# Token 0 first through the feed-forward block, and the step index read earlier

## The reference, cut to what matters

```
def step(h, p):
    op = jnp.argmax(h[0, 0, :NOPS])                      # NOPS = 19
    q = h @ p['wq'][op]; k = h @ p['wk'][op]; v = h @ p['wv'][op]
    attn = softmax(einsum('bqd,bkd->bqk', q, k) * scale)
    y = einsum('bqk,bkd->bqd', attn, v) @ p['wo'][op]
    h = where(p['am'][op], y, h)
    z = relu(h @ p['w1'][op] + p['b1'][op]) @ p['w2'][op] + p['b2'][op]
    h = where(p['fm'][op], z, h)
```

## Time and profile before

| | us |
|---|---|
| median of 3 runs (lowest to highest) | 219.69 (218.63 to 220.36) |
| the profiled execution, its device time | 218.97 |
| the profiled execution, its span | 217.2 |
| TensorE products busy in the span | 171.0 (79%) |
| VectorE busy | 142.4 (66%) |
| ScalarE busy | 107.8 (50%) |
| POOL busy | 58.3 (27%) |

### The profile page before, as it was taken

The page is one execution under the profiler, slowest core; times in us unless marked ns, Lnnn a source line. Parts: engine busy times, 40 slices in busy tenths (PEclk is TensorE's granted clock), DMA queues, the critical chain, the costliest instruction groups (busy, mean ns, idle before and its releaser), DMA issues.

```text
span 217.2 us, 4109 instructions
## 1 busy us (share of the span) xinstructions
PE 171.0 (79%) x1197; PEld 116.4 (54%) x1199; DVE 142.4 (66%) x392; ACT 107.8 (50%) x318; POOL 58.3 (27%) x136
## 2 busy tenths in 40 slices
PE   8589969965594799989369499999684999998730
PEld 5554856532392577745242278677332787765310
DVE  0862265857957688893844478898755589787452
ACT  2334261237853566662577058676441576755330
POOL 8800000000060545561000004654600036555100
PEclk9999999999769589999956969999997599999985
DMA  6500000000000000000000000000000000000002
GB/s 210 199 0 3 0 3 1 2 0 5 0 0 0 3 0 3 0 0 0 10 11 6 18 0 0 0 0 0 0 0 14 0 0 0 0 0 0 0 0 98
DMA packets 2635, 3.18 MB, mean 15 GB/s; under 512 B 825, under 2 KB 1849, under 8 KB 2618
## 3 DMA queue, kind: packets, MB, share of 16 engines
q1 hardware_dynamic: 2330, 2.66, 3.9%
q10 hardware_dynamic: 288, 0.32, 0.5%
HBM read 2.45 MB, written 0.53 MB: 14 GB/s over the span
## 4 chain that ended last, share of the span: by engine, by line
PE 55%; DVE 19%; ACT 8%; issue 8%; DMA 3%; POOL 3%; DVEq 2%; ACTq 1%; SPq 1%; POOLq 0%
PE bank L502 15%; PE bank L475 8%; PE bank L489 4%; PE bank L466 4%; PE bank L728 4%; ACT qz L890 3%; PE bank L562 3%; PE bank L616 3%; PE bank L545 3%; DVE big L1168 3%; POOL prob L418 3%; DMA kx<-kx_dram 2%; DVE minus L1152 2%; DVE filt L331 2%; PE bank L766 2%
## 5 line engine op out<-in xcount | busy, mean ns | idle before, releaser
L418 POOL TENSOR_SCALAR prob<-prob,einv 128x256 f32<-128x256 f32 x96 | 44.9, 482 | 62.6 <-DVE einv L1163 62.6
L1168 DVE COPY big<-bank 128x512 f32<-128x512 f32 x48 | 32.9, 686 | 6.2 <-PE bank L475 6.1
L475 PE MATMUL bank<-ident,prob 128*128 128x128 f32 x192 | 31.2, 286 | 6.9 <-POOL prob L418 6.8
L807 ACT ACTIVATE prob<-bank,nmax 128x256 f32<-128x256 f32 x64 | 29.8, 472 | 12.8 <-DVE nmax L1155 12.8
L502 PE MATMUL bank<-hT,qz 128*128 128x256 f32 x128 | 33.6, 391 | 0.0
L475 PEld LDWEIGHTS bank<-ident,prob 128*128 128x128 f32 x192 | 22.2, 144 | 19.5 <-POOL prob L418 15.3
L502 PEld LDWEIGHTS bank<-hT,qz 128*128 128x128 f32 x128 | 23.2, 198 | 4.1 <-issue 1.6
L1155 DVE TENSOR_REDUCE nmax<-bank 128x2 f32<-128x512 f32 x32 | 21.7, 687 | 5.1 <-PE bank L502 4.6
L807 ACT ACTIVATE prob<-minus,nmax 128x256 f32<-128x256 f32 x32 | 15.9, 499 | 10.9 <-DVE nmax L1152 8.3
L502 PE MATMUL bank<-kt,qz 128*128 128x256 f32 x64 | 18.4, 419 | 3.2 <-ACT prob L807 3.2
L545 PE MATMUL bank<-ident,filt 128*128 128x128 f32 x96 | 12.2, 276 | 5.1 <-DVE big L1003 2.1
(11 more groups left out here) (161 smaller groups left out, 253.6 us busy)
## 6 DMA issues: line engine op xcount, KB each, us to landing
xrev<-xrev_dram SPq DMA_DIRECT2D x1, 512.0 KB, 5.3
xin<-xtok_dram SPq DMA_DIRECT2D x1, 512.0 KB, 5.2
out_dram<-outT SPq DMA_DIRECT2D x2, 256.0 KB, 2.3
wx<-wx_dram SPq DMA_DIRECT2D x1, 288.0 KB, 4.0
maskc<-maskc_dram SPq DMA_DIRECT2D x1, 256.0 KB, 4.9
kx<-kx_dram ACTq DMA_DIRECT2D x1, 248.0 KB, 4.1
constf<-constf_dram SPq DMA_DIRECT2D x1, 218.0 KB, 5.3
wa<-wa_dram SPq DMA_DIRECT2D x3, 56.0 KB, 1.8
```

The lines of the kernel that those rows point to most:

```text
L418: last = nc.gpsimd.tensor_scalar(prob[b % NPB][:, ih, :], prob[b % NPB][:, ih, :], einv[:, b, ih:ih + 1], 1.0, ALU.mult, ALU.mult)
L475: mm = pe.transpose(bank[2 + b % 2][:, jh * S + ih * P:jh * S + (ih + 1) * P], prob[b % NPB][:, ih, jh * P:(jh + 1) * P], ident)
L807: e = nc.scalar.activation(prob[b % NPB][:, ih, :], scores, ACT.Exp, bias=nmax[:, b, ih:ih + 1], scale=-1.0 if masked else 1.0, accum_out= ...
L1168: nc.vector.tensor_copy(flat(probT[b % NTB]), bank[2 + b % 2][:, :]).then_inc(s_PT, 1)
```

## The change

- A single column of the hidden layer, token 0's, is multiplied first, into column 0 of bank 7 (`TOKEN0`), ScalarE applies ReLU to it into a new tile `h0`, and TensorE multiplies `h0` with `w2` and adds the bias into columns 32 to 63 of bank 7, behind the first half of the hidden products. Three semaphores order this.
- `pick_op` on VectorE stands ahead of its ReLUs of both halves.
- The second half's fourth hidden product uses bank 7 (the third bank 3), and waits until VectorE has copied the row.
- TensorE calls `next_step` after the second half and ahead of the output products. VectorE calls it ahead of its last drain.
- ScalarE drains groups 0, 1 and 2, VectorE group 3 alone.

```diff
-        FF = "ADAD" + "ADAD" + "ADAD"
+        FF = "ADAD" + "ADAD" + "AAAD"
-        HBANK = ((0, 1, 4, 2), (5, 6, 7, 3))
+        HBANK = ((0, 1, 4, 2), (5, 6, 3, 7))
+        TOKEN0 = bank[7]
...
                     for q in range(GB):
                         rows = slice(q * C, (q + 1) * C)
+                        if (gp, q) == (1, GB - 1):
+                            pe.wait_ge(s_rowc, r)
                         pe.matmul(bank[HBANK[gp][q]][:, :], w1r[rows, :], flat(hT[rows, 2 * gp:2 * gp + 2, :]),
...
+                    pe.matmul(TOKEN0[:, 0:1], w1r[0:C, :], hT[0:C, 0, 0:1], start=True, stop=True,
+                              tile_position=(0, 0)).then_inc(s_h0, 1)
                     hidden(t, k0, 0)
+                    ffns = pe.snap(reg_ffns)
+                    pe.wait_ge(s_h0r, ffns)
+                    pe.matmul(TOKEN0[0:1, C:2 * C], h0[:, 0:1], w2s, start=True, stop=False)
+                    pe.matmul(TOKEN0[0:1, C:2 * C], b2s, ident[:, 0:C], start=False, stop=True).then_inc(s_row, 1)
+                    pe.reg_alu(reg_ffns, reg_ffns, 1, ALU.add)
...
                     hidden(t, k1, 1)
-
-                    t.drained(pe, k0 + 1)
-                    pe.matmul(bank[0][0:1, 0:C], relu[:, 0, 0, 0:1], w2s, start=True, stop=False)
-                    pe.matmul(bank[0][0:1, 0:C], b2s, ident[:, 0:C], start=False, stop=True).then_inc(s_row, 1)
+                    next_step(pe, b, reg_r, reg_op, reg_code)
                     for n in range(NG):
...
                         mm.then_inc(s_task, 1)
-                    next_step(pe, b, reg_r, reg_op, reg_code)
                     weight_products()
...
                     act.wait_ge(s_w1z, r)
+                    ffns = act.snap(reg_ffns)
+                    act.wait_ge(s_h0, ffns)
+                    nc.scalar.activation(h0[:, :], TOKEN0[:, 0:1], ACT.Relu, bias=b1s).then_inc(s_h0r, 1)
+                    act.reg_alu(reg_ffns, reg_ffns, 1, ALU.add)
...
-                    for n in (0, 2):
+                    for n in (0, 1, 2):
                         t.filled(act, k + n)
...
-                link(nc.vector.tensor_copy(row[:, :], bank[0][0:1, 0:C]))
+                nc.vector.tensor_copy(row[:, :], TOKEN0[0:1, C:2 * C]).then_inc(s_rowc, 1)
+                dve.wait_ge(s_rowc, r)
                 argmax_op(row[:, 0:NOPS])
...
+                    pick_op(r)
                     k = k0
                     for gp in range(2):
...
-                        if gp == 0:
-                            pick_op(r)
                         k += GB
-                    for n in (1, 3):
-                        t.filled(dve, k + n)
-                        nc.vector.tensor_scalar(hT[:, n, :], bank[ZBANK[n]][:, 0:S], b2s, None, ALU.add).then_inc(s_dd, 1)
                     next_step(dve, b, reg_r, reg_op, reg_code)
+                    n = NG - 1
+                    t.filled(dve, k + n)
+                    nc.vector.tensor_scalar(hT[:, n, :], bank[ZBANK[n]][:, 0:S], b2s, None, ALU.add).then_inc(s_dd, 1)
```

More of the change, by code:

```diff
@@ L200, in build @@
         wfs = sb("wfs", [HID, C + 2])
+        h0 = sb("h0", [HID, 1])
         w2s, b1s, b2s = wfs[:, 0:C], wfs[:, C:C + 1], wfs[:, C + 1:C + 2]
@@ L231, in build @@
             "step_weight_products_in_psum"), sem("step_block_weights_ready")
+        s_h0, s_h0r, s_rowc = sem("token0_hidden_in_psum"), sem("token0_hidden_ready"), sem("token0_copied")
         s_fin = sem("out_ready")
@@ L661, in _ @@
             pe.reg_mov(reg_att, B)
-            reg_wp = pe.alloc_register("pe_weight_products")
+            reg_wp, reg_ffns = pe.alloc_register("pe_weight_products"), pe.alloc_register("pe_ffns")
+            pe.reg_mov(reg_ffns, 1)
             pe.reg_mov(reg_wp, 0)
@@ L788, in _ @@
                     pe.wait_ge(s_dd, dd)
-                    pe.matmul(bank[0][0:1, 0:C], hT[:, 0, 0:1], ident[:, 0:C], start=True, stop=True).then_inc(s_row, 1)
+                    pe.matmul(TOKEN0[0:1, C:2 * C], hT[:, 0, 0:1], ident[:, 0:C], start=True, stop=True).then_inc(s_row, 1)
                     next_step(pe, b, reg_r, reg_op, reg_code)
@@ L917, in _ @@
             act.reg_mov(reg_task, len(STATIC))
+            reg_ffns = act.alloc_register("act_ffns")
+            act.reg_mov(reg_ffns, 1)
             reg_code, reg_op, reg_step, reg_kind, reg_r = (
```

## The result

The changed kernel takes **212.41 us** (median of 4 runs, 211.73 to 213.28) beside 220.01 (218.63 to 220.36) for the kernel before, a ratio of 0.967 [0.961, 0.972]. The forecast was 213.8, range 211.8 to 217.2. The profiled execution of the changed kernel took 213.28, its longest of four, with a span of 211.5; that of before 218.97, span 217.2. Both have 1.8 us outside the span, so the rows account for 5.7 us, and the rest of the 7.6 between the medians is which executions were profiled.

The account below looks back on a forecast made before the run. TensorE work set more than half of the span, with hollows where it waited for the late index. Gains of 1.3, 2.0 and 2.0 plus 0.6 for the clock, 5.9 us, off the median 219.69 gave 213.8, range 211.8 to 217.2.

Parts of the forecast that it names:

- Block 2: Second feed-forward block and change of step: earlier index lets weight products start 2.0 us earlier, directly behind the output products.
- The end: Last drain to final addition: drain 1.0 us earlier and VectorE's reading, taken as 1.0, no longer behind it; 2.0.
- TensorE's reading is covered: TensorE's register reads ahead of the outputs, taken as 1.0 us, hide behind its second half and VectorE's ReLU.
- the bound of 4.5: First half's output products starting later than 4.5 us after the block's first product would mean TensorE's reading isn't covered.
- The uncovered rival: TensorE reads registers only after the second half leaves the array, for 1.48 us: sum 2.7, 217.0 us; chance 0.13.
- its slower form: TensorE's reading takes longer than POOL's 1.48 us, each microsecond more costing three: 222.3 us; chance 0.05.
- VectorE's registers hold the diagonals: Changes of step: queries stay 2.55 us behind VectorE's last drain, 1.0 later in both: 215.8 us; chance 0.10.
- The clock: TensorE's half clock in attentions behind the blocks: busier TensorE holds full clock partly, a credit of 0.6 us.
- a hollow of 0.9: TensorE's idle gap remaining in front of the queries' products, a reason to take the clock credit nearer to zero.
- The bound of 1.9: Most a held clock could give back over both half-clock stretches, 0.65 + 1.21 us.
- Block 1: First feed-forward block, at half clock: earlier index brings the weight products forward, a gain of 1.3 us.
- The gain is given back: Later first outputs and a clock falling inside the second half lose 1.7 us in blocks 2 and 3: 217.8; chance 0.05.

Follow-up runs that it names:

- both_back: The changed kernel with TensorE's and VectorE's reading of the step both behind their last work again: 219.2 us, ratio 0.986.
- before_dve: The kernel before with only VectorE's reading of the step moved ahead of its last drain: 217.55 us, ratio 0.993.
- pe_back: The changed kernel with TensorE's reading of the step back behind the output products: 216.07 us, ratio 0.988.
- dve_back: The changed kernel with VectorE's reading of the step back behind its last drain: 217.81 us, ratio 0.993.
- again2: The changed kernel, unaltered, timed and profiled a further time: 212.35 us, ratio 0.973.
- tok_behind: The changed kernel with token 0's hidden product behind the first half's four products instead of ahead: 212.75 us, ratio 0.973.
- mix: The changed kernel with token 0's hidden product behind the first half in block 1 alone, ahead in blocks 2 and 3: 213.55 us, ratio 0.971.
- pick_back: The changed kernel with the index again between VectorE's ReLUs of the two halves: 216.46 us, ratio 0.989.
- mix_warm: The kernel of mix with 20 spare TensorE products ahead of block 1, meant to hold the clock: 213.73 us, ratio 0.974.

## Why the prediction was right

**Block 2, 2.0 forecast, 2.35 measured.** Counted from the first product, second outputs were forecast at 5.58 and came at 5.64, weight products at 6.65 and came at 6.64. From both_back, 0.93 of it is the early index with the second ReLU behind it, and 3.69 - 3.38 = 0.31 the load that is no longer late; 3.38 - 2.27 = 1.11 are the two readings. The working kept 1.60 from the weight products to the queries; it is 1.27 now, and that is the surplus. It is the clock's: the four weight products take 0.71 and not 1.22, while before_dve, with VectorE's registers out of the way but the weight products at half clock, keeps 1.60.

**The end, 2.0 forecast, 2.03 measured**: the drain 0.94 earlier (forecast 0.99), VectorE's reading 1.09 (taken as 1.0); before_dve gives 1.10 for it alone.

**TensorE's reading is covered**, as forecast with 1.0 of cost: it ended at 162.05, inside the second half, and outputs of the first half came at 4.31 behind the first product, before the bound of 4.5. Taking it away again (pe_back) moves them to 4.04 and leaves the second outputs where they are. The uncovered rival and its slower form are out.

**VectorE's registers hold the diagonals**, a rival with 0.10: it had the queries stay 2.55 behind the last drain, and they came 1.13 behind it. But dve_back shows the mechanism at full size where VectorE's reading stands behind the drain, so the change itself removes it. The forecast priced VectorE's reading at the end alone. In the changes of step the gain came by the load and TensorE in the working; in truth it needs both readings gone. From the second outputs to the queries it is 3.21 in pe_back, 3.39 in dve_back, 3.38 in both_back and 3.62 in before_dve, against 2.27 with neither in the way.

**The clock, 0.6 forecast, 1.49 measured** (1.45 behind block 2, 0.04 behind block 1). The step that was mis-sized: I took a hollow of 0.9 in front of the queries as enough to leave most of the fall in place. The rows show it gone behind block 2 in the changed kernel and in its repeats, and the whole stretch at 32.55 to 32.58. The bound of 1.9 was drawn too low as well, since it ended at the copies of the queries: 0.39 of the 1.45 lie behind them, and the weight products' surplus above lies ahead. What made the clock hold stays open. In both_back, where TensorE still waits 0.6 and 1.0 us around the weight products, it held too (32.56); in pe_back and dve_back it fell for 3.41 us (33.33 and 33.35). Behind block 1 it depends on the execution: 33.34 where it fell (124.55 to 127.95), 32.52 in again2 where it held. The Trainium skill, "TensorE: Matmul & The Clock Gate", Terms, prices throttled time at that time multiplied by one minus the granted share. For the 6.83 us behind block 2 that is an estimated 3.4; the trace disagrees, with 1.45 in the attention, 1.06 of it up to the copies of the queries, and some 0.33 ahead of it.

**Block 1, 1.3 forecast, a loss of 0.67 measured**: the step that failed. The working put the row's copy 2.42 behind the block's first product; it came at 3.92. The copy stands 0.41 behind the row's product, so that product was due at 2.01 and came at 3.51. Of these 1.50, 0.97 are the one-column product ahead of the half: the half ends at 2.44 without it (tok_behind), so it costs 1.07, and I had priced it by its own length, 0.1. Moved behind the half it gives back only 0.67, since TensorE then waits 0.39 for ScalarE's ReLU. The other 0.53 are the half itself, 2.44 against the 1.91 that I had read from two halves in a row, which overlap: in the trace of before the first ends at 2.27 and the second starts at 1.87. From there on it grows. The index is 1.22 late. Both ReLUs stand behind it (118.20 to 120.93) while before the first ran under TensorE's second half, and the second outputs come 7.96 behind the first product (6.53 forecast, 7.03 before). Last, the load took 3.0 us and held the weight products for 0.43, where 0.4 of slack had been forecast: they come at 9.69 instead of 7.62.

So the forecast is 5.9 as a sum of 1.3, 2.0, 2.0 and 0.6, measured -0.67, 2.35, 2.03 and 1.49: 5.2, with 0.51 more from ahead of the blocks. Block 1 fell short by 2.0; the clock and block 2 gave 1.2 more. The two large terms, block 2 and the end, are hit by their mechanism; that the total came as near is luck, since the misses of block 1 and of the clock have opposite signs. By the medians the gain is 7.6 and not 5.9; the repeats, with 0.975 and 0.973, put it at 5.4 and 5.9.

**The gain is given back** (0.05) was seen in part: it put the fall of the clock inside the second half. In mix, pe_back, dve_back, both_back and pick_back it fell in the first 0.7 us of block 2 or 3 in the profiled execution, which made that block some 1.5 us longer. In the changed kernel's three profiles it did not. One profile each can't tell whether the edits or chance brought this.

## What to carry to other kernels

A scalar that decides the next step should be computed ahead of the bulk work of the same engine, and every engine's reading of it put where that engine waits anyway. Two engines that read registers at the same moment hide one another: in block 2, moving one reading alone gained 0 to 0.2 us (before_dve, pe_back, dve_back), both together 1.1, so cost such readings jointly. A reading can be covered by the array's work only if what it reads is there in time (pick_back). What is laid ahead of a group of tiles that run side by side must be priced by what it does to their overlap.

## What was not expected of the hardware

- **A product of one column can delay four tiles.** With it in the first row group, the eight products of block 1 that share the array by tiles took 3.2 to 3.6 us at half clock instead of 2.1 to 2.7. At full clock it costs 0.2 (1.33 instead of 1.14), and the row is multiplied 1.27 behind the block's first product with it ahead, 1.64 with it behind. Half clock alone does not explain block 1: in both_back's block 3, where the clock fell 0.2 us in, the eight took 2.34 with it ahead. Why they fall out of step in block 1 stayed open.
- **A load is slow when an instruction packet travels beside it.** Block 1's weight load took 3.0 us from issue to landing, block 2's 1.7. The traffic around it in the changed kernel:

```profile
q1 hardware_dynamic: 192, 0.07, 10.3%
q8 instruction: 1, 0.02, 2.6%
wa<-wa_dram SPq DMA_DIRECT2D x1, 56.0 KB, 3.0
```

In eight of the nine profiles where TensorE reads the step ahead of the outputs, an instruction packet (q8) left 0.5 us after the load's issue, and the load took 2.5 to 3.0. In the five where it reads behind them, the packet left 1.3 to 3.1 us before, and the load took 1.7 to 1.8. The ninth, mix_warm, separates the packet from the order of the code. It reads ahead too, has no such packet beside the load, and its load is a fast one:

```profile
q1 hardware_dynamic: 192, 0.07, 14.1%
wa<-wa_dram SPq DMA_DIRECT2D x1, 56.0 KB, 1.7
```

The first load of `wa`, ahead of block 1, does the same within one kernel: 2.9 us in the changed kernel with a q8 packet 0.6 after the issue, 1.7 in again2 without one. Over all 42 loads of the 14 profiles, the 16 with a q8 packet (16 KB) in their first 0.8 us took 2.2 to 3.3, the other 26 1.7 to 2.0, with or without one of the 8 KB packets of queue q14. How the packet slows the load isn't shown.
- **Where the clock rises in block 1 varies** between executions with the same work: 121.1, 130.2 and 120.9 in the changed kernel's three profiles. The late rise cost little there: from block 1's first product to the end it is 98.51 us, against 98.45 in the first. What decides it stayed open.
